# The last stage of a graph and expert network: gate groups, load slots and output rows rearranged

## The reference

```python
# ... agg: attention of the edges, summed per node; ee = exp(e - e_max), denom = segment sum of ee
scores = _layernorm(agg, ln_gamma, ln_beta).reshape(M, HEADS, NUM_EXPERTS).mean(1)
topk_s, topk_i = jax.lax.top_k(scores, TOP_K)
w = jax.nn.softmax(topk_s, axis=-1)
out = jnp.zeros_like(x)
for ei in range(NUM_EXPERTS):
    g = jnp.where(topk_i == ei, w, 0.0).sum(-1)
    hh = jax.nn.gelu(x @ W1[ei] + b1[ei], approximate=False)
    out = out + g[..., None] * (hh @ W2[ei] + b2[ei])
# x = x + out
```

## Time and profile before

| | us |
|---|---|
| median of 3 runs | 4529.32 |
| lowest and highest run | 4510.36, 4531.97 |
| profiled execution | 4518.21 |
| its span, first to last instruction | 4516.4 |
| start of `finale` in it (first DMA of SP) | 4215.6 |

### The profile page before, as it was taken

One profiled execution on the slowest core, in us unless ns is written; L12 is line 12 of the kernel. 1 busy time (PEld: TensorE's weight loads), 2 busy tenths in 40 slices (PEclk: granted clock), 3 DMA queues, 4 the chain that ended last, 5 costly groups with the idle time before them and its releaser, 6 DMA issues. The chain is left out here.

```text
span 4516.4 us, 41418 instructions
## 1 busy us (share of the span) xinstructions
PE 3385.8 (75%) x11935; PEld 2249.1 (50%) x11935; DVE 2489.3 (55%) x6314; ACT 982.0 (22%) x1993; POOL 3133.5 (69%) x3120
## 2 busy tenths in 40 slices
PE   6588888888788898555555576999999999920374
PEld 3364455555455565333333374666666666610243
DVE  8747766666678667665444461343334333422476
ACT  6662222222100000000000163222222222200132
POOL 4417777777777777777777476777777777777650
PEclk9899999999988888777787556999999999965687
DMA  8454444444444654333334776443443434222578
GB/s 218 138 134 148 126 132 128 130 131 127 131 139 131 170 148 126 104 105 103 101 102 99 102 240 167 113 122 109 129 118 109 136 116 116 72 63 63 115 179 214
DMA packets 243164, 582.31 MB, mean 129 GB/s; under 512 B 69794, under 2 KB 126663, under 8 KB 238062
## 3 DMA queue, kind: packets, MB, share of 16 engines
q0 software_dynamic: 134096, 314.40, 26.5%
q1 hardware_dynamic: 108841, 265.25, 20.3%
HBM read 440.04 MB, written 139.27 MB: 128 GB/s over the span
## 5 line engine op out<-in xcount | busy, mean ns | idle before, releaser
L1044 POOL DMA_INDIRECT g_rows<-table,gcn_srcT x1664 | 1679.7, 1009 | 517.8 <-issue 485.0
L1110 PE MATMUL g_ps<-g_rows,g_hot 128*125 128x256 f32 x3328 | 1043.0, 457 | 478.2 <-issue 272.1
L1939 POOL DMA_INDIRECT n_rows<-gtab,so_own x1122 | 1091.0, 972 | 342.1 <-issue 342.1
L1382 DVE TENSOR_TENSOR acc<-acc,g_ps 125x256 f32 x1664 | 697.9, 419 | 745.5 <-PE g_ps L1110 608.4
L1110 PEld LDWEIGHTS g_ps<-g_rows,g_hot 128*125 128x125 f32 x3328 | 699.9, 224 | 788.5 <-issue 443.0
L1880 PE MATMUL p_ph<-f_xfT,f_w 128*128 128x500 f32 x1408 | 604.1, 585 | 30.3 <-DMA f_xfT<-xfT_d 30.3
L1886 PE MATMUL p_py<-f_w,f_hh 128*125 128x256 f32 x2816 | 618.6, 379 | 0.0
L1886 PEld LDWEIGHTS p_py<-f_w,f_hh 128*125 128x125 f32 x2816 | 528.5, 188 | 105.9 <-issue 28.8
L2082 DVE TENSOR_TENSOR keep<-p_py,keep 125x512 f32<-125x512 f32 x176 | 121.2, 692 | 737.1 <-PE p_py L1886 736.7
L1880 PEld LDWEIGHTS p_ph<-f_xfT,f_w 128*128 128x128 f32 x1408 | 268.6, 191 | 328.2 <-issue 322.9
L2110 ACT ACTIVATE f_hh<-p_ph,f_b 128x500 f32<-128x500 f32 x352 | 232.0, 677 | 644.8 <-PE p_ph L1880 644.5
(11 more groups left out here) (347 smaller groups left out, 3784.9 us busy)
## 6 DMA issues: line engine op xcount, KB each, us to landing
o_d<-keep SPq DMA_DIRECT2D x19, 1920.0 KB
keep<-o_d SPq DMA_DIRECT2D x14, 1920.0 KB
g_rows<-table,gcn_srcT POOLq DMA_INDIRECT x1664, 2.8
n_rows<-gtab,so_own POOLq DMA_INDIRECT x1122, 2.5
gout<-n_o SPq DMA_DIRECT2D x33, 408.0 KB
xnT_d<-a_xnT SPq DMA_DIRECT2D x25, 500.0 KB, 2.9
m_area<-xnT_d SPq DMA_DIRECT2D x25, 500.0 KB, 3.7
qT_d<-m_area SPq DMA_DIRECT2D x25, 500.0 KB, 3.0
```

Of the source, the lines that this page charges most:

```text
L1044: pool.indirect_dma_start(out=rows[:, g % RING, j], out_offset=None, in_=K.table, in_offset=bass.IndirectOffsetOnAxis(ap=K.gcn_srcT[:, 4 * ...
L1110: mm = pe.matmul(ps[q, p % 4, b], hot[:, g % 4, 2 * j + b], rows[:, g % RING, 2 * j + b], start=True, stop=True, skip_group_check=True)
L1382: dve.tensor_tensor(a, a, ps[q, p % 4, b], ALU.add).then_inc(add_s, 1)
L1939: pool.indirect_dma_start(out=rows[:, c % 3, j], out_offset=None, in_=K.gtab, in_offset=bass.IndirectOffsetOnAxis(ap=K.gat_src[:, c * W + ...
```

## The change

The five groups become six: 76 to 83 (blocks 19 and 20 alone), 84 to 99 (block 21 and the late blocks), 0 to 7, 8 to 23, 24 to 47, 48 to 75. By `due` the first stands ahead of R0, the second ahead of R1, the third ahead of U1, the fourth (new) ahead of U2, the fifth ahead of R8 and the sixth ahead of U8. R2 now needs the second group, R3 and R4 the third, R5 to R8 the fourth. ACT makes the first group's root and exponential between the gelu of U0 and that of U1. `more` gets two slots, so there are five in all (SLOTS_IN = 5): R3 and R4 are loaded when the first group's sums have landed, R5 behind R0's store, and so on. `part` is no tensor of its own any more but a view of `so_x`, which held edge lists in earlier stages and has 16 KB per partition, of which the ring takes 12.

```diff
+MORE = 2
...
-    RING, SLOTS_IN = 3, KEEP + 1
-
-    spans = [((EARLY - KEEP) * SUB, EARLY * SUB), (EARLY * SUB, NT), (0, 24), (24, 48), (48, (EARLY - KEEP) * SUB)]
+    RING, SLOTS_IN = 3, KEEP + MORE
+
+    kept = (EARLY - KEEP) * SUB
+    spans = [(kept, kept + 2 * SUB), (kept + 2 * SUB, NT), (0, 8), (8, 24), (24, 48), (48, kept)]
...
-        more = m.sb("z_more", [P, SUB, NE, D])
-        part = m.sb("z_part", [P, RING, SUB, D])
+        more = m.sb("z_more", [P, MORE, SUB, NE, D])
+        part = K.so_x[:].rearrange("p b c -> p (b c)")[:, 0:RING * SUB * D].rearrange("p (r j f) -> p r j f", r=RING, j=SUB)
...
-            return K.keep[:, (EARLY - KEEP + at) % KEEP] if at < KEEP else more[:]
+            return K.keep[:, (EARLY - KEEP + at) % KEEP] if at < KEEP else more[:, at - KEEP]
...
                 sp.wait_ge(summed[0], 16 * (spans[0][1] - spans[0][0]))
-                load_early(KEEP)
+                for i in range(KEEP, SLOTS_IN):
+                    load_early(i)
...
-                        act.wait_ge(in_o[i % SLOTS_IN], 32 * (i // SLOTS_IN + (i % SLOTS_IN == KEEP)))
+                        act.wait_ge(in_o[i % SLOTS_IN], 32 * (i // SLOTS_IN + (i % SLOTS_IN >= KEEP)))
...
-                for n in range(min(2, parts)):
-                    gelu(0, n)
+                gelu(0, 0)
+                roots(0)
+                gelu(0, 1)
                 for at, (kind, i) in enumerate(order):
                     for g in due(at):
-                        roots(g)
+                        if g:
+                            roots(g)
```

## The result

The changed kernel takes 4495.53 us (median of 6 runs, 4486.38 to 4504.82), the kernel before, run beside it, 4518.25 (6 runs, 4510.36 to 4531.97). The ratio is 0.9946, 95% interval 0.9926 to 0.9966: 22.7 us less by the medians. The profiled execution took 4497.4 us, 20.8 less than that of before; its span is 4495.7. All of it lies in the last stage: it began at 4215.9 (before 4215.6) and took 279.8 us instead of 300.8.

A forecast was written before the change was run, and what follows sets the result against it. Transfers were taken as the bound in the last stage: 21.7 us from 5.2 MB less plus 3.3 us at the start, minus 3 at the end, gives 22 us, 4529.3 to 4507 us; range 4484 to 4533.

The forecast's parts named there:

- Start: First group in the last stage: loads of R3 and R4 issued at 4227.5, R0 weighed at 4249.9 instead of 4254.4.
- Second group: 16 tiles: starts at 4254.4 after a 9.2 us gather landing, between 4249.9 and 4259; the start's 4.5 us are lost.
- Rival 1: Gathers land early, second group starts at 4250, everything behind is 4.5 us earlier: 28 to 36 us won; chance 0.16.
- Third group: 8 tiles: DVE enters at 4279.4 without waiting, leaves at 4288.6, 18.8 us earlier; R3's store 18.5 us earlier.
- the walk: The prediction's step-by-step timeline of the last stage, from the first group to the end, giving 22 us won.
- Fourth group: 16 tiles, 4302.7 to 4314.3: PE waits until 4317, U4 ends at 4348.4 instead of 4352.9; 4.5 us left there.
- SP: SP's 18.0 us wait for the first late output stays, ending at 4348.5; after 4362 DMA waits 6 us for R8.
- Signs: Right: DMA share over 0.7 from 4294 to 4316; wrong: second group after 4259, or share under 0.85 behind 4370.
- Sum: 5.2 MB less at 240 GB/s, 21.7 us, plus 3.3 us earlier start, 25.0, less 3 for the end: 22 us.
- Rival 2: Late units set the end, so freed transfers only wait later: about 5 us won, 0 to 12; chance 0.26.
- late units* theory: Gelu, PE and DVE's late units set the end; gelu ahead of the root would win 10 to 20 us more.
- Rival 3: Slower: second group beyond 4259 makes U4 later than before; 9.6 us late, the kernel loses 5; chance 0.08.

## Why the prediction was right

The forecast was 22 us less, 4507 off the median and 4496 off the profiled execution; measured were 22.7 us by the medians of runs side by side and a profiled execution of 4497.4. The median that the forecast started from was itself 11 us above the one of the larger set, so the step of taking the gain off it was the poorer of the two. In brackets below is what was forecast.

- *Start*: loads at 4227.70 (forecast 4227.5), R0 weighed at 4247.9 (4249.9). Right, and, as forecast, lost at the second group; the run with the late root shows it.
- *Second group*: 4257.01 against 4254.4, inside the bounds of 4250 and 4259. The landing was mis-sized: 11.54 us, not 9.2. The cause was named rightly (the loads in flight), and the run with the later load shows it. Rival 1 falls with its condition, a start at 4250.
- *Third group*: no wait, 4282.05 to 4290.6, R3's store at 4299.91: 2 us behind the walk, all from the second group.
- *Fourth group*: 4304.5 to 4315.8; PE stood 10.22 us; U4 ended at 4349.7 (4348.4), and R8's store left at 4369.0 (4368).
- *SP*: released at 4355.05, not 4348.5, so the hole lies ahead of the release and not ahead of R8. Its size was right, 6 us.
- *Signs*: the DMA share from 4294 to 4316 is 0.84, over the 0.7 named. From 4370 to the end of the span it is 0.82, under the 0.85 that was to mean that the late units have taken over; but before the change it was 0.84 there too, so that sign could tell nothing.
- *Sum*: from R8's store to the span's end 126.7 us, forecast 126.4. The last 30 us carried 121 GB/s x 30 = 3.6 MB, which at 243 would take 15 us: 15 lost. In the last 56.3 us before, 10.8 MB would have taken 45: 11 lost. By this estimate the end cost 4 us where I took 3.

One step was wrong, and the total hides it; that the sum came out so close is in part luck. I counted the fifth slot as one load less, 8.5 us of the 25, and let its load at the start cost only what the second group's landing would take in any case. The run with four slots has the same ratio, 0.9945, without the slot: it gains those 8 us at the second group instead. The slot alone, on the old groups, is worth 6 us; on top of the small third group nothing that these runs can measure. What carries the change is the six groups, and in them, by the table, above all the third one of 8 tiles.

Rival 2, 0 to 12 us, lies outside the measured interval, which is 15 to 33 us. That transfers are the bound is supported by the rate in the long stretch (240 GB/s before, 243 after) and by the late units that came 9 us earlier without the 10 to 20 us that the *late units* theory asked for. It is not shown to be the whole truth: edits that filled further holes showed no gain that the intervals can tell. Why the stretch behind R8 gives back what was won ahead of it stays open. One rival was not tested: the ring of three row buffers, which no run changes. ACT waits for a store to land before it can make the next first product, 10.44 us at the longest, and that wait stands on the chain that ended last, ahead of the last group; behind 4369 DVE stands 12.2 us in all for such products. Rival 3 did not come about: the second group started 2 us before its point, 4259.

## What to carry to other kernels

Look for the stretch in which the bounding resource stands idle and ask which one step opens it; here a group of 24 tiles was gated as a whole although the next transfer needed 4 of them, and the finer groups alone, among them the first 8 cut off, gave the whole gain that was measured. Before another buffer is filled early, see what else is in flight: the load that it lets go ahead delays the small transfers that the next step waits for, and the two can cancel. Where several parts of a change are to share a gain, run each alone, since a sum can be right with a term in it wrong.

## What was not expected

Gathers of 128 short rows fared far worse behind large loads than I took them to. The Trainium skill, page "DMA: Bandwidth & Descriptors", section "Queues, rings and completion order", says that each DMA engine takes turns between its queues packet by packet, by which one would not expect a gather to sit out a whole load of another queue. The runs show a landing of 11.54 us with R3's and R4's loads in flight, and one of 2.7 us where R3's load was through when the gather started. That a gather waits until the loads ahead of it are over fits both, but no run shows it by itself.

And a DVE that weighed earlier held up gathers that it then had to wait for: 0.95 us a gather, but 8.41, 11.03 and 6.35 us for three of them in the run with the later load and the gelu ahead. Long gathers as such are not new. The rows shown ahead of the prediction have 4.76 us at most, but the same trace has this one, later in the stage, where DVE did not have to wait for it:

```profile
4329.16 8.41 POOL L2276 DMA_INDIRECT gsum<-gout,gat_last  x1 [0.30 <-issue]
```
